# A deformable-convolution block in fp32: column sums for the biases, a shorter normalisation chain, and later places for a border fill, a clamp and some stores

## The reference, cut to what matters

```python
def block(x, ...):                       # x: (8, 32, 128, 128) fp32
    x = x + L0(_gn(x), ...)              # _gn: group norm, 32 groups = each channel by itself
    x = x + L1(_gn(x), ...)
L0: depthwise 3x3 conv, then three 32x32 channel mixes (two of them softmax weights)
L1: off    = conv3x3(x, w_off)                       # 64 channels of offsets
    mapped = bilinear gather of x at (grid + off)    # rows and columns clipped to the image
    out    = conv3x3(mapped, w_conv) + b_conv
```

## Time and profile before

| | us |
|---|---|
| three runs: lowest, median, highest | 812.98, 816.37, 818.92 |
| the profiled execution | 817.38 |
| its span, first to last instruction | 815.6 |
| chunk 0 of image 0 starts on PE at | 58.3 |
| chunk 0 of image 1 | 133.87 |
| chunk 0 of image 2 | 225.45 |
| chunk 0 of image 6 | 608.85 |
| chunk 0 of image 7 | 701.30 |
| mean granted clock of TensorE, share of full speed | 0.965 |
| queues of SP and ACT together, share of the 16 DMA engines | 67.9% |

### The profile page before, as it was taken

How to read it: one execution, slowest core, us unless ns; L and a number is a source line. 1 busy time by engine, 2 the same in 40 slices (tenths; PEclk the granted TensorE clock), 3 DMA queues, 4 the chain that set the end, 5 groups by cost and what they waited for, 6 DMA issues and landing times. The chain is left out here.

```text
span 815.6 us, 9297 instructions
## 1 busy us (share of the span) xinstructions
PE 739.2 (91%) x2780; PEld 287.6 (35%) x2780; DVE 538.6 (66%) x1047; ACT 468.5 (57%) x821; POOL 489.7 (60%) x432
## 2 busy tenths in 40 slices
PE   4799965999999799998999799998999989978984
PEld 4343322333343243333433233332433334323321
DVE  4685896559952898528983589628995386526741
ACT  7477756655663656645564754637557455556720
POOL 4015966764593765736767365956657468668950
PEclk9999987999999899999999999999999999998997
DMA  8939436597479874989649794697749442675464
GB/s 145 189 72 182 99 68 143 93 172 152 95 177 173 165 146 92 222 133 182 138 119 219 143 191 86 152 198 165 146 94 216 96 105 62 155 130 130 108 146 106
DMA packets 215816, 114.27 MB, mean 140 GB/s; under 512 B 142448, under 2 KB 208080, under 8 KB 212176
## 3 DMA queue, kind: packets, MB, share of 16 engines
q1 hardware_dynamic: 192192, 101.96, 59.6%
q10 hardware_dynamic: 23568, 11.65, 8.3%
HBM read 16.91 MB, written 16.78 MB: 41 GB/s over the span
## 5 line engine op out<-in xcount | busy, mean ns | idle before, releaser
L1225 DVE COPY_PREDICATED other_row<-down_ps,row_diff 128x768 f32<-128x768 int32 x128 | 123.7, 1020 | 194.2 <-ACT down_ps L862 194.2
L1041 POOL TENSOR_TENSOR other_row<-other_row,x_quads 128x512 f32<-128x512 f32 x64 | 76.0, 1187 | 229.0 <-DVE other_row L1237 228.9
L659 PE MATMUL off_ps<-x1a,wo 128*128 128x512 f32 x384 | 187.8, 626 | 20.1 <-DVE other_row L1237 14.2
L562 PE MATMUL c_ps<-mapb,w 128*64 128x512 f32 (+1 forms) x384 | 179.1, 609 | 16.1 <-ACT x1a L810 12.2
L562 PE MATMUL c_ps<-xb,w 128*64 128x512 f32 (+1 forms) x384 | 170.8, 592 | 6.0 <-DMA xb<-xa 3.0
L564 PE MATMUL c_ps<-xa,w 128*64 128x512 f32 x384 | 175.8, 605 | 0.0
L659 PE MATMUL off_ps<-x1b,wo 128*128 128x512 f32 x384 | 175.2, 592 | 0.0
L564 PE MATMUL c_ps<-mapa,w 128*64 128x512 f32 x336 | 162.2, 626 | 0.0
L851 ACT ACTIVATE other_row<-row_diff 128x768 f32<-128x768 f32 x128 | 101.6, 842 | 88.3 <-POOL row_diff L1027 72.5
L659 PEld LDWEIGHTS off_ps<-x1a,wo 128*128 128x128 f32 x384 | 70.3, 196 | 131.2 <-issue 109.6
L659 PEld LDWEIGHTS off_ps<-x1b,wo 128*128 128x128 f32 x384 | 72.6, 189 | 92.4 <-issue 92.4
(11 more groups left out here) (122 smaller groups left out, 854.8 us busy)
## 6 DMA issues: line engine op xcount, KB each, us to landing
x1b<-x1a SPq DMA_DIRECT2D x28, 520.0 KB, 6.7
mapb<-mapa SPq DMA_DIRECT2D x28, 520.0 KB, 6.7
mapa<-mapped SPq DMA_DIRECT2D x224, 64.0 KB, 2.1
xb<-xa SPq DMA_DIRECT2D x26, 520.0 KB, 8.2
out_dram<-x1a SPq DMA_DIRECT2D x49, 256.0 KB, 4.7
x_quads<-x1a SPq DMA_DIRECT2D x192, 65.0 KB, 2.2
xa<-in_x_dram ACTq DMA_DIRECT2D x40, 256.0 KB, 7.5
xa<-in_x_dram SPq DMA_DIRECT2D x16, 256.0 KB, 7.0
```

The costliest lines, as they stand in the source:

```text
L562: nc.tensor.matmul(bank[0:64, n0:4 * W], weights[:, kx, :], rows_b[:, b0:4 * g + 4, kx:kx + W], start=(kx == 0), stop=(kx == 2))
L659: last = nc.tensor.matmul(off_ps[k % 2][:, CH * n:CH * n + CH], wo[wpar][:, kx, :], rows[:, 4 * k:4 * k + 4, kx:kx + W], start=(kx == 0), ...
L1041: step(pool.tensor_tensor(split(column), split(column), own, ALU.add))
L1225: last = dve.copy_predicated(other_row[n][:, :, KR // 2 * odd:KR // 2 * odd + KR // 2, :], bass.AP(tensor=rows.tensor, offset=rows.offset ...
```

## The change

It has seven parts.

1. The three taps of each weight are added once (`w1_sum`, `wo_sum`, `w2_sum`), and `norm`'s callers multiply the mean by 1 / deviation (`scaled_x`, `scaled_1`). A bias is then one matmul for each half of the partitions, in place of three.
2. `norm` aggregates first within each partition (48 numbers), gathers only the mean and the variance, and combines four of each. One product of a Newton step is written as a tensor_scalar.
3. ACT's `pad_x1(i, ., 1)` moves from chunk 0 to chunk 1, and `clamp(i, 1)`, with `pad_end`, from chunk 1 to chunk 2.
4. `CONV2_SETUP` goes from 3 to 2, and ACT takes the bias b2 behind the groups x1 of its chunk.
5. `END_CONV2` takes one group more of image 6 in chunk 5 and so leaves one for the end where there were two.
6. The store of the first half of image 5 is moved from the end of image 6's turn on SP to behind `copy_mapb(1)` of image 7; the two halves of image 6 each wait for their own groups.
7. The last image is stored group by group, in turn from SP and from ACT.

```diff
-    END_CONV2 = [[], [], [0], [1], [], [2], [3, 4], [5]]
+    END_CONV2 = [[], [], [0], [1], [], [2, 3], [4, 5], [6]]
-    CONV2_SETUP = 3
+    CONV2_SETUP = 2
...
-            def mean_sum(bank, col, weights, mean):
+            def mean_sum(bank, sums, scaled):
                 last = None
                 for t in range(2):
-                    for kx in range(3):
-                        last = nc.tensor.matmul(bank[64 * t:64 * t + 64, col:col + 1], weights[:, kx, :], mean[:, :],
-                                                start=(kx == 0), stop=(kx == 2))
+                    last = nc.tensor.matmul(bank[64 * t:64 * t + 64, 0:1], sums[:, :], scaled[:, :],
+                                            start=True, stop=True)
...
             def norm(stats, mean, rstd, mean_ready):
+                settle(apart=True)
+                step(dve.bn_aggr(own_mv[:, :], stats[:, :, :]))
+                settle()
                 for q in range(4):
-                    step(dve.tensor_copy(stats_c[:, q, :, :], stats[Q * q:Q * q + Q, :, :]))
+                    step(dve.tensor_copy(four_mv[:, :, q], own_mv[Q * q:Q * q + Q, :]))
                 settle(apart=True)
-                step(dve.bn_aggr(mv[:, :], stats_c[:, :, :, :]))
+                step(dve.bn_stats(four_stats[:, :], four_mv[:, 0, :]))
+                step(dve.reduce_sum(var_sum[:, :], four_mv[:, 1, :], AX))
+                settle(apart=True)
+                step(dve.bn_aggr(mv[:, :], four_stats[:, :]))
+                step(dve.tensor_scalar(var_eps[:, :], var_sum[:, :], 0.25, EPS, ALU.mult, ALU.add))
                 settle()
-                step(dve.tensor_scalar(var_eps[:, :], mv[:, 1:2], EPS, None, ALU.add))
+                step(dve.tensor_scalar(var_eps[:, :], var_eps[:, :], mv[:, 1:2], None, ALU.add))
...
-                    step(dve.tensor_tensor(rs[:, :], rs[:, :], newton[:, :], ALU.mult))
+                    step(dve.tensor_scalar(rs[:, :], rs[:, :], newton[:, :], None, ALU.mult))
...
                 norm(stats_x, mean_x[par], rstd_x, x_mean)
+                step(dve.tensor_tensor(scaled_x[par][:, :], mean_x[par][:, :], rstd_x[:, :], ALU.mult))
                 if isinstance(i, int) and i == 0:
                     dve.wait_ge(s_setup["pool"], 4)
+                    sum_columns(w1_sum, w1_base)
...
-                    if prev and k == 0:
+                    if prev and k == 1:
                         pad_x1(i, i % 3, 1)
-                    if k == 1:
+                    if k == 2:
                         clamp(i, 1)
...
+            def store_group(queue, i, par, g, rows=(1, 2, 3, 0)):
+                image = out[i].rearrange("c (b r) w -> c b r w", r=4)
+                b, e = 4 * g, 4 * g + 4
+                for q in rows:
...
-            for piece in range(2):
-                sp.wait_ge(out_ready, 8 * (NB - 1) + 7 + piece)
-                store_end(NB - 1, (NB - 1) % 3, piece)
+            for m in (1, 3, 5):
+                sp.wait_ge(out_ready, 8 * (NB - 1) + m + 1)
+                store_group(sp, NB - 1, (NB - 1) % 3, END_GROUPS[m])
+            sp.wait_ge(out_ready, 8 * NB)
+            store_group(sp, NB - 1, (NB - 1) % 3, END_GROUPS[7], (1, 2))
...
-            act.wait_ge(out_ready, 8 * (NB - 1) + 6)
-            store(act, NB - 1, (NB - 1) % 3, 0)
+            for m in (0, 2, 4, 6):
+                act.wait_ge(out_ready, 8 * (NB - 1) + m + 1)
+                store_group(act, NB - 1, (NB - 1) % 3, END_GROUPS[m])
+            act.wait_ge(out_ready, 8 * NB)
+            store_group(act, NB - 1, (NB - 1) % 3, END_GROUPS[7], (3, 0))
```

More of the change, by code:

```diff
@@ L275, in stored_count @@
         def stored_count(part, images):
-            pieces = 4 if part == 1 and not (isinstance(images, int) and images < NB) else 0
-            return DMA * (STORES[part] * images + pieces)
+            before = images if isinstance(images, int) and images < NB else images - 1
+            return DMA * STORES[part] * before
+        END_STORES = DMA * (4 * 8 + 1)
         def xa_of(i):
@@ L313, in move_quads @@
                                               1 + c0:1 + c1]).then_inc(quad_x1[half], DMA)
+        def store_group(queue, i, par, g, rows=(1, 2, 3, 0)):
+            image = out[i].rearrange("c (b r) w -> c b r w", r=4)
+            b, e = 4 * g, 4 * g + 4
+            for q in rows:
+                first = 1 if q == 0 and g == 0 else 0
+                n, r = (b - 1, 3) if q == 0 else (b, q - 1)
+                queue.dma_start(image[:, n + first:n + 4, r, :], x1a[par][Q * q:Q * q + Q, b + first:e, 1:W + 1])\
+                     .then_inc(end_stored, DMA)
+            if g == 0:
+                queue.dma_start(image[:, BL - 1:BL, 3, :], x1a[par][0:Q, BL:BL + 1, 1:W + 1]).then_inc(end_stored, DMA)
         def store(queue, i, par, part):
@@ L467, in _ @@
                         sp.wait_ge(out_ready, 8 * (i - 1))
-                        store(sp, i - 2, (i - 2) % 3, 1)
+                        for part in range(2):
+                            store(sp, i - 2, (i - 2) % 3, part)
                     sp.wait_ge(end_pads, 1)
@@ L611, in offsets_bias @@
                 pe.wait_ge(wo_ready, i + 1)
[L612 to L615 removed]
+                nc.tensor.matmul(ps[:, 0:1], wo_sum[:, :], scaled_1[par][:, :], start=True, stop=True)\
+                  .then_inc(bo_summed, 1)
             def conv2_bias(i, wpar, par, ps):
                 pe.wait_ge(w2_ready, i + 1)
[L619 removed]
+                mean_sum(ps, w2_sum, scaled_1[par]).then_inc(b2_summed, 1)
             def conv2(i, wpar, m, ps):
@@ L914, in _ @@
                         pad_x(i + 2, i % 2)
-                    if prev and k == (CONV2_SETUP if nxt else END_SETUP):
-                        conv2_bias(i - 1, (i - 1) % 2, bank("b2", i - 1, 0))
-                    if not nxt and k == END_BIAS + 1:
-                        conv2_bias(i, i % 2, bank("b2", i, 0))
                     groups = conv1_groups(i, k)
@@ L924, in _ @@
                         x1_group(i + 1, (i + 1) % 2, (i + 1) % 3, m, i + 1 >= 3, bank("x1", i + 1, m))
+                    if prev and k == (CONV2_SETUP if nxt else END_SETUP):
+                        conv2_bias(i - 1, (i - 1) % 2, bank("b2", i - 1, 0))
+                    if not nxt and k == END_BIAS + 1:
+                        conv2_bias(i, i % 2, bank("b2", i, 0))
                     for half in range(2):
```

57 lines of the change are left out of this document (35 added, 22 removed).

## The result

The changed kernel took 769.61 to 772.67 us in four runs, median 772.49; the kernel before, beside it on the same chip, 812.98 to 818.92, median 815.81. The ratio is 0.946, with a 95% interval from 0.9418 to 0.9501. The forecast was 773 us. The profiled execution took 772.33 us, its span is 770.5.

A forecast was written before the change was run, and what follows sets the result against it. PE was taken to bound the kernel wherever it runs without a gap. Span 815.6 - 32.9 - 2.0 - 2.5 - 3.5 - 2.5 = 772.2 us, 774.0 for the profiled execution, forecast 773 us; range 757 to 797.

The forecast's parts named there:

- The bound and the stand of ACT: Images 2 to 6: PE bounds; moving clamp and border fill later ends ACT's 10.57 us wait; with other terms, -32.9 us.
- The matmul sets: Bias matmuls in every image: shorter sets save PE 1.1 us an image, bounds 0 and 1.7.
- a wait of 0.8 for DVE: Images 2 to 6: PE's wait for DVE's addition, kept at 0.8 us an image in the pitch.
- The norm: Two norms at the end of image 0, where DVE leads: 1.25 us gained each, -2.5 us, bounds +2 and -7.
- The rule of the Trainium skill: Norm's copies: two-port copies and SBUF tensor_tensors block until GpSimd's instruction ends; norm term about -0.5, sum 775.
- Image 7: PE's last wait, for the end moves on SP's queue: moves start 3.5 us earlier, -3.5 us (+1.6 to -5.1).
- The tail: Last addition to the span's end: the smaller last store, split over two queues, starts at once, -2.5 us (0 to -4).
- DVE becomes the bound: Rival, images 2 to 6: two norms 3.5 us longer an image, +17.5, 790 us; chance 0.14.
- The wait moves with the clamp: Rival at chunk 2: x1_quads lands 6 us later, ACT stands still again, 792 to 800 us; chance 0.10.
- the 2 us named as a sign: Expected in the changed profile: ACT's idle time before the second clamp is under 2 us.
- Slower: Rival, 14 norms in images 1 to 7: small DVE instructions wait on POOL, 5 us more each, 836 us; chance 0.03.

The follow-up runs named there:

- u_sums: The changed kernel with three matmuls on the unscaled weights for each bias in place of one on their sum: 776.12 us, ratio 0.9518.
- the pair with long sets: Two variants of the changed kernel with three matmuls for each bias: with the new norm 776.12 us, with the old norm 775.71 us.
- norm_plus12: The changed kernel with twelve more small tensor_scalar instructions in each norm, 2.2 us, their results unused: 816.76 us, ratio 0.9997.
- e6_share: The changed kernel with part 6 undone and half of the end's second set of moves issued from ACT: 770.64 us, ratio 0.9447.

## Why the prediction was right, and where its terms were not

**The bound and the stand of ACT.** Right, and shown from both sides. A full image of PE with short sets was worked out as 88.9 - 1.1 = 87.8 us; one number a copy, which has no waits, shows 87.3. Parts 3 and 4 alone bring 443.8 for five images where 5 x 88.9 = 444.5 had been worked out for PE without a wait. That the forecast of 773 lies within 1 us of 772.49 is in part luck: the terms missed by 1 to 2 us each, with 3.7 us too much hoped for in images 0 and 1 and the last groups, and 5.3 too little in images 2 to 6, image 7 and the tail.

**Part 4.** The prediction priced parts 3 and 4 as one, and rightly: alone, part 3 leaves a gap of 0.93 us an image, and part 4 takes 6.8 us more by the medians (in the two profiles images 1 to 6 are 5.3 shorter with it). Of this, 1.15 us are image 1's.

**The matmul sets.** The mechanism was right and the size of a set too (0.23 instead of 0.60), but the term was mis-sized: not 1.1 an image but 0.5, 3.6 us for the whole kernel. The prediction subtracted 1.1 and kept a wait of 0.8 for DVE as a thing of its own. The two hang together: without the short sets the wait is all but gone, and with them it is 0.7 on average. (Of the 3.6 us, 1.7 lie ahead of image 0 in the profile of u_sums.) The pitch of 88.6 that the two gave together is near the 88.15 measured for that reason.

**The norm.** The step that failed is the 1.25 us a norm, between waiting and not waiting. The copies wait as before, and the term was -1.2 at image 0 instead of -2.5. Image 0 lasts 75.6 to 75.7 us in all four kernels with the old norm and 74.3 in all six with two numbers a copy and nothing added; with one number a copy it is 73.6, and 71.9 where the scaled products don't wait either. In the total of the pair with long sets the new norm gave nothing. The rule of the Trainium skill weighed in the prediction (SBUF — State Buffer, Who interferes with whom, with VectorE: DVE Perf Modes, Mode 2×_2P — use both read ports for one tensor) made this term about -0.5 in the prediction's working, and the traces agree with it in each kind: copies of two numbers up to 1171 ns, of one number 147 at most, the tensor_tensor product 1.16 us beside a `row_diff`. By this rule the term is 0.7 off and by the forecast 1.3; the sum by the rule, 775, is 2.5 us above 772.5, and the forecast 0.5, since other terms were off too.

**Image 7.** -5.0 where -3.5 was said, and the term was put together wrongly. The prediction had SP lead, with 3.8 us won by taking the five stores away from the turn and 3.3 to 10 lost to them later. SP's moves did start earlier, 44.4 us after image 7's first chunk where it was 50.4, but parts 1 to 4 without the moved stores bring the -5.0 as well (79.9), and the time at which PE goes on is the same with and without part 6. What was not predicted is that PE itself came to this wait far earlier, so that it grew and the clock fell behind it: against before, where it was 0.91, 1.3 us given back in the last groups, and 2.9 against the kernel without part 6. The prediction had put this at nothing.

**The tail.** -4.1 instead of -2.5, just past its bound of -4. No run has part 7 alone, so its size rests on parts 5 to 7 together (11.35 us from PE's end without them, 7.3 with parts 5 and 7) and on the table above.

**The rivals.** *DVE becomes the bound* did not happen, and its price was right: it had 3.5 us more of norms an image at 17.5 us for the five images, and norm_plus12 shows 22.7 for 4.4. *The wait moves with the clamp*: a little of it did, 8.5 us in five places altogether, two of them over the 2 us named as a sign (2.10, 2.35), and PE did not wait for it. *Slower*: its mechanism is real, its price was too low. It had put the point from which the gain is used up at 3.5 us a norm; 2.2 us bring the kernel back to 0.9997, since PE waits nearly in full, its clock falls behind the wait, and the three norms ahead of image 0 cost 7.2 us that had not been counted.

What stays open: why e6_share's end rows come as late as they do, what makes the norm ahead of image 0 begin 1.1 to 1.7 us later in some kernels, and how the tail's gain is divided between parts 5 and 7. None of these was tried.

## What to carry to other kernels

When an engine in the middle of a pipeline stands at a wait that only a later step needs, the loss is what is queued behind it; move the wait to just ahead of its user, and look at once for the small gap that takes its place (here a bias in the shared banks, 6.8 us). The terms of one sum are not independent where an engine is ahead of another by less than a microsecond: shortening its work there mostly lengthens its wait, as the short sets show, which gave nothing in images 2 to 6 as long as ACT stood at the clamp. And one long wait of TensorE can cost more than several short ones of the same sum (7.89 against four that add up to 7.8, 2.9 us), since the clock falls behind the long one.

## What the runs showed of the hardware that was not expected

Small VectorE instructions differ by form in whether they wait beside GpSimd, and not by size: copies of 32x2 fp32 have a mean of 547 ns and a most of 1171, copies of 32x1 137 and 147, and a tensor_scalar with a column as operand 200 to 202 in 48 instances. So twice as many copies can be half the time. A large tensor_scalar is not safe: the one of 128x384 took 1.47 us beside `row_diff`, 0.41 elsewhere. No run tried counts other than 1, 2 and 48.

The 84 matmul instructions behind TensorE's last wait can be compared in twelve kernels, and the length of that wait does not by itself set what it costs:

| last wait (us) | granted clock of the groups behind it | time of the 84 (us) |
|---|---|---|
| 1.31, 1.90 | 1.00, 1.00 | 16.6 |
| 2.93, 2.96, 3.02 | 0.91, 0.91, 0.91 | 18.1 to 18.3 |
| 3.30 | 0.85 | 19.6 |
| 4.25, 6.54, 7.53 | 0.86, 0.90, 0.85 | 18.3 to 19.5 |
| 7.89, 7.95, 9.09 | 0.85, 0.91, 0.89 | 18.2 to 19.4 |

The two short waits cost nothing. All the others cost 1.5 to 3 us, one of 3.30 as much as one of 7.89, and 7.95 less than 7.89. Why the clock comes back sooner in one kernel than in another is not shown.

Issuing one store on SP's queue took 0.4 to 2.0 us in the kernel after, and three of the same shape 5.99 us at 695.87 and 2.41 at 704.45. The DMA engines were 95% busy in the first stretch and 82% in the second; whether that makes the difference, no run shows.
